# Expert rows added into the result by DMA, filler products in the first routing, later transposes, root degrees spread by a load: one graph transformer kernel on one core

## The chip, the cores and the metric

The kernel runs on one NeuronCore of one Trainium2 chip. The metric is the device time of one execution in microseconds (us). The kernel before was timed three times: 1880.01, 1882.05 and 1882.09 us, median 1882.05. One further execution was profiled.

## The reference, cut to what matters

There are N = 1250 nodes with C = 768 features and 20000 edges. Two layers are computed. Each adds to x a graph part and an attention part, both from the normalised x, and then a mixture of experts on the normalised result:

```
xn = layernorm(x)
x = x + gat(xn, edges) + linear_attention(xn)            # layer 0
x = x + experts0(layernorm(x))     # 8 experts, 2 per row, out = sum of gate * (row @ W_e + b_e)
xn = layernorm(x)
x = x + gcn(xn, edges) + l2_attention(xn)                # layer 1
x = x + experts1(layernorm(x))     # 8 experts, 2 per row, with a hidden layer and gelu
```

In `gcn` the row of every node is scaled by 1/sqrt(degree), on the source side and on the destination side. In `l2_attention` q and k are normalised over the nodes, so that their sums over all nodes are wanted beside them.

## The kernel before, in words

The 1250 rows are 10 tiles of 125 rows (`NT`, `T`). `X` holds x in SBUF, `XN` three normalised tiles, `XT` the transposed normalised rows. Work is written out by hand for each engine; semaphores tie them. `plan_jobs` numbers the jobs that go through PSUM and gives each a bank in turn and the engine that empties it; TensorE's `begin(m)` waits until the job that last had the bank was emptied. SP issues nearly all loads, in order; `load(u)` fills one of two weight slots of 2304 KB.

**Order in time.** Layer 0's k, v, q and projection run to 430 us, the graph part of layer 0 (units of two heads and some tiles, VectorE lines 1867 and following) to 728 us. During that part the tiles 0 to 7 are normalised for the experts (`normal(1, t)`), tiles 8 and 9 right after it (`LATE`).

**First routing** (`route`, TensorE L1020, VectorE L1901). VectorE picks two experts of each row; TensorE counts ranks (L1026 to L1028), VectorE makes from them the place of each row among tiles of 128 rows that belong to one expert, TensorE gathers the row numbers of each place into `TOK` (L1034, 20 products behind VectorE's L1956). `TAB` holds the expert of each tile and the numbers of turns. Between its products TensorE has nothing to do. With these inputs there are 25 tiles: 12 turns of two and one over.

**First experts** (TensorE L1042 `turn`, L1066 `expert0`). For tile n POOL gathers 128 normalised rows from DRAM (`gather`, L611, L622) into one of two buffers `XG`. TensorE transposes them (L1054), ScalarE copies them to `XGT` (L1404), TensorE multiplies by the expert's weights (L1076, 12 matmuls, which the profile shows as 24 passes). VectorE adds the bias to `YS` (L2011), ScalarE stores the 128 rows to DRAM in `expert_rows` (`store`, L1411). POOL forms the index of the gather itself: a multiplication (L614), a drain, a cast (L616), a drain, the indirect DMA (L622). After the last tile POOL gathers for every node tile the two rows of `expert_rows` that belong to its nodes (L657, 20 gathers, four buffers `YG`), and VectorE adds them to `X` with their gates `GW` (`weighted`, L2017), takes the statistics (L1578 to L1586) and normalises the tile (L1590, L1600) once ScalarE has the root (L1246).

**Next stage.** TensorE sums the degrees (L1099, L1104), transposes tiles 0 and 1 (L721) and computes q in five chunks of 250 nodes, six groups of 128 columns each (L1117, 12 passes a group); in each chunk, after three groups, it transposes the two tiles of the next chunk. A chunk waits until ScalarE has copied its two tiles. Then k and v follow (L744). VectorE has made for each tile a diagonal matrix `DG` of 1/sqrt(degree), and TensorE multiplies ones by it (L1126), which spreads the values over all partitions; VectorE copies them to `DB` (L2080). Then comes the projection (L734 with `QK`), whose start waits until VectorE has emptied v's last job.

**Second experts** (L1186, L1208). Here the gates are applied in place: twenty products (L1221) bring the three bf16 parts of the gates and the row numbers to each place, VectorE sums them (`GTE`, `SIDX`, L2165 to L2172), forms `YS` = gate * bias (L2000) and `YS` += gate * product (L2005), and POOL adds the rows of `YS` into the result in DRAM by an indirect DMA with addition (`add_rows`, L668). The indices of the gathers are made by VectorE (L2158). Two adds never run together: each waits for the one before it to land.

Of the kernel before, what the change touches and what calls it, by code (L numbers as in the profile page):

```python
# [13 lines left out]
P = 128  # L14
N = 1250
# [62 lines left out]
YB = {1: 4}  # L78
# [25 lines left out]
def plan_jobs():  # L104
# [27 lines left out]
    for L in (1, 2, 3):  # L132
# [34 lines left out]
def graph_transformer(nc, xn_d, y_d, x, src, dst, gW, gWT, gWresT, attnT, w0, wp0, bp0, rwT, rb, ewT, eb,  # L167
# [6 lines left out]
    def sb(name, shape, dt=F32):  # L174
# [35 lines left out]
    IDXA = sb("IDXA", [T, KT], U32)  # L210
# [135 lines left out]
    TVG = sb("TVG", [T, KT, 4, ETC], BF16)  # L346
    GTE = sb("GTE", [P, ETC])
    SIDX = sb("SIDX", [P, ETC])
    cursor[0] = eb_base
# [5 lines left out]
    YS = sb("YS", [P, 2, C])  # L355
    assert cursor[0] <= at_base
# [12 lines left out]
    YG1 = sb("YG1", [T, YB[1], C])  # L369
    assert cursor[0] <= top - XNB * C * 4  # L370
    cursor[0] = yg_base
# [22 lines left out]
    DG = sb("DG", [T, NT, T])  # L394
    assert cursor[0] <= top - XNB * C * 4
# [8 lines left out]
    consts = sem("consts")  # L404
# [17 lines left out]
    tn_filled, tn_emptied, lr_filled, lr_emptied, lg_filled, lg_emptied, dg_ready = (sem(s) for s in (  # L422
        "tn_filled", "tn_emptied", "lr_filled", "lr_emptied", "lg_filled", "lg_emptied", "dg_ready"))
# [4 lines left out]
    y_cleared = sem("y_cleared")  # L428
# [5 lines left out]
    yg_in, yg_used = [sem(f"yg_in{b}") for b in range(YB[1])], sem("yg_used")  # L434
    gate_parts, gates_full, gates_in, ys_ready, acc_in, idx_ready = (sem(s) for s in (
        "gate_parts", "gates_full", "gates_in", "ys_ready", "acc_in", "idx_ready"))
# [37 lines left out]
    def _(sp):  # L474
# [64 lines left out]
        spare = 2 * N // P * P  # L539
        sp.dma_start(y_d[spare:, :], x[0:ET_MAX * P - spare, :]).then_inc(y_cleared, 16)  # L540
# [6 lines left out]
        for u, (c, p) in enumerate(UNITS):  # L547
# [3 lines left out]
            if u >= RSLOTS:  # L551
                sp.wait_ge(w_ready, 20 * (u - RSLOTS + 1))
            sp.dma_start(RBS[u % RSLOTS][:, :, 0:nt * T],
                         rows_d[2 * p:2 * p + 2, t0 * T:(t0 + nt) * T].partition_broadcast(T)).then_inc(rb_in[u % RSLOTS], 16)
        sp.wait_ge(fin_dve, len(UNITS))
# [21 lines left out]
        for t in range(NT):  # L577
            sp.wait_ge(dve_emptied, J.emptied("dve", J.at[f"agg2_{t}"] + 1))
            sp.dma_start(out[t * T:t * T + PA, :], X[0:PA, t, :]).then_inc(acc_in, 16)
            sp.dma_start(out[t * T + PA:(t + 1) * T, :], X[PA:T, t, :]).then_inc(acc_in, 16)  # L580
# [7 lines left out]
        sp.wait_ge(acc_in, 32 * NT)  # L588
# [3 lines left out]
    def _(pool):  # L592
# [48 lines left out]
        with nc.gpsimd.Fori(0, n) as i:  # L641
            for a in range(2):
                pool.wait_ge(turned_n[1], i * 2 + a + 2)
                gather(1, i * 2 + a + 2, a)
        with nc.gpsimd.Fori(0, over) as j:
            pool.wait_ge(turned_n[1], n * 2 + j + 2)
            gather(1, n * 2 + j + 1, 0)

        pool.wait_ge(xg_in[1][0], (n + over) * 16 + 16)
        pool.wait_ge(xg_in[1][1], n * 16 + 16)  # L650
        pool.wait_ge(ys_out[1][0], (n + over) * 16 + 16)
        pool.wait_ge(ys_out[1][1], n * 16 + 16)
        nc.gpsimd.sem_inc(y_all, 1)
        for q in range(KT):
            if q >= YB[1]:
                pool.wait_ge(yg_used, q - YB[1] + 1)
            nc.gpsimd.indirect_dma_start(out=YG1[:, q % YB[1], :], out_offset=None, in_=y_d,  # L657
# [1569 lines left out]
```

## Time and profile before

| what | value |
| --- | --- |
| median of three runs | 1882.05 us |
| the profiled execution's own time | 1882.65 us |
| its span (first to last instruction) | 1880.7 us |
| mean granted clock of TensorE | 0.972 |
| TensorE busy | 1769.1 us (94%) |
| VectorE, ScalarE, POOL busy | 725.2, 392.5, 134.1 us |
| TensorE, share of the chain that ended last | 84% |
| bytes moved by DMA | 142.22 MB |

A page or an answer of the trace gives times in us from the first instruction, and durations of single instructions in us or ns. PE is TensorE, PEld its weight loads, DVE VectorE, ACT ScalarE, POOL GpSimd, SP the engine that issues loads; L with a number is a line of the kernel. The granted clock is a share of 2.4 GHz: 1.00 or 0.50, between them for a stretch with both. In the chain that ended last, each piece is what released the piece after it.

### The profile page before, as it was taken

How to read it: one execution, taken by the hardware profiler on the slowest of the kernel's cores; microseconds unless marked ns; L12 is line 12 of the kernel's file. 1: busy time of each engine (PE TensorE's matmuls, PEld its weight loads, DVE VectorE, ACT ScalarE, POOL GpSimd, SP SyncE). 2: the span in 40 equal slices, each digit the busy share in tenths (PEclk: the TensorE clock that was granted, in tenths of full speed). 3: DMA queues.
4: the chain of work that ended last, by engine and by line, in shares of the span. 5: the costliest groups of instructions: out<-in, count | busy, mean ns of one | idle time of the engine just before them, and what ended most of it. 6: DMA issues, size and time to landing. Idle time of an engine off the chain costs nothing.

```text
span 1880.7 us, 24731 instructions
## 1 busy us (share of the span) xinstructions
PE 1769.1 (94%) x7994; PEld 1090.2 (58%) x7995; DVE 725.2 (39%) x1826; ACT 392.5 (21%) x1034; POOL 134.1 (7%) x169
## 2 busy tenths in 40 slices
PE   7999999999999986899997999999999999779997
PEld 4555555554333343566666855555569669756664
DVE  4321545756789887211116211151111114432222
ACT  2441221113322222011013321000221221122221
POOL 0000000000000000111114000000000000013322
PEclk9999999999999998899998999999999999879999
DMA  6001101001001114355536011010010012535772
GB/s 196 1 0 62 68 24 39 1 1 36 30 23 49 34 42 182 95 200 190 195 130 190 30 51 51 0 51 0 0 51 1 0 50 84 193 105 139 198 196 40
DMA packets 53582, 142.22 MB, mean 76 GB/s; under 512 B 10079, under 2 KB 20723, under 8 KB 53045
## 3 DMA queue, kind: packets, MB, share of 16 engines
q1 hardware_dynamic: 34053, 87.05, 13.4%
q0 software_dynamic: 11952, 34.05, 7.5%
q10 hardware_dynamic: 7488, 19.93, 3.0%
q8 instruction: 56, 0.92, 0.2%
q14 instruction: 33, 0.27, 0.0%
HBM read 113.69 MB, written 33.99 MB: 79 GB/s over the span
## 4 chain that ended last, share of the span: by engine, by line
PE 84%; DVE 8%; issue 2%; DMA 2%; DVEq 2%; ACT 1%; ACTq 0%; POOL 0%; SPq 0%; POOLq 0%
PE PS L734 21%; PE PS L1076 10%; PE PS L744 8%; PE PS L1186 5%; PE PS L1208 5%; PE PS L842 4%; PE PS L876 4%; PE PS L1158 4%; PE PS L1144 4%; PE PS L1117 4%; PE PS L982 3%; DVE WRA L1867 3%; PE PS L823 2%; PE PS L1054 2%; PE PS L991 2%
## 5 line engine op out<-in xcount | busy, mean ns | idle before, releaser
L734 PE MATMUL PS<-WS,XT 128*125 128x384 f32 x960 | 313.6, 488 | 1.4 <-issue 1.4
L734 PEld LDWEIGHTS PS<-WS,XT 128*125 128x125 f32 x960 | 180.5, 189 | 129.5 <-issue 3.6
L1076 PE MATMUL PS<-WS,XGT 128*128 x600 | 199.4, 490 | 0.0
L1076 PEld LDWEIGHTS PS<-WS,XGT 128*128 128x128 f32 x600 | 113.1, 192 | 74.4 <-issue 2.0
L744 PE MATMUL PS<-XT,WS 128*128 128x416 f32 (+1 forms) x432 | 151.2, 512 | 0.0
L1867 DVE SCALAR_TENSOR_TENSOR WRA<-RB,U,AT 125x500 f32<-125x500 f32 (+1 forms) x240 | 140.0, 645 | 2.2 <-PE PS L991 0.6
L744 PEld LDWEIGHTS PS<-XT,WS 128*128 128x128 f32 x432 | 81.6, 189 | 69.2 <-issue 69.2
L982 PE MATMUL PS<-WRA,F 125*64 125x500 f32 (+1 forms) x480 | 100.7, 531 | 9.7 <-DVE WRA L1867 8.6
L1186 PE MATMUL PS<-WS,XGT 128*128 x288 | 99.4, 496 | 1.5 <-ACTq L1406 1.1
L2011 DVE TENSOR_TENSOR YS<-PS,EBB 128x768 f32<-128x768 f32 x25 | 23.9, 957 | 191.2 <-PE PS L1076 191.2
L1208 PE MATMUL PS<-WS,HT 128*128 x276 | 92.9, 486 | 1.0 <-DVE YS L2005 1.0
L1404 ACT ACTIVATE XGT<-PS 128x384 f32<-128x384 f32 x102 | 44.5, 488 | 222.8 <-DVE YS L2011 176.2
L876 PE MATMUL PS<-WS,QT 128*125 128x384 f32 x240 | 82.8, 499 | 0.0
L842 PE MATMUL PS<-XT,WS 128*128 128x416 f32 (+1 forms) x216 | 80.4, 525 | 0.5 <-DVEq L1730 0.5
L1117 PE MATMUL PS<-XT,WS 128*128 128x250 f32 x360 | 79.4, 382 | 0.6 <-issue 0.6
L626 POOL DMA_INDIRECT XG<-xn_rows,IDX x25 | 27.6, 1104 | 724.9 <-DVEq L1962 619.1
L1481 ACT ACTIVATE HF<-PS,DT 125x384 f32<-125x384 f32 x40 | 23.2, 581 | 263.0 <-PE PS L734 263.0
L734 PE MATMUL PS<-WS,QK 128*125 128x384 f32 x240 | 77.6, 486 | 0.0
L2094 DVE TENSOR_TENSOR HH<-HF,HH 125x384 fp32r<-125x384 f32 x40 | 22.3, 558 | 136.5 <-ACT HH L1483 136.5
L1117 PEld LDWEIGHTS PS<-XT,WS 128*128 128x128 f32 x360 | 69.5, 194 | 9.4 <-issue 1.0
L1186 PEld LDWEIGHTS PS<-WS,XGT 128*128 128x128 f32 x288 | 53.9, 194 | 35.0 <-issue 4.0
L1208 PEld LDWEIGHTS PS<-WS,HT 128*128 128x128 f32 x276 | 52.4, 190 | 37.6 <-issue 1.3
(319 smaller groups left out, 2149.6 us busy)
## 6 DMA issues: line engine op xcount, KB each, us to landing
WS<-in_ewT SPq DMA_DIRECT2D x8, 2304.0 KB, 10.6
WS<-in_fW SPq DMA_DIRECT2D x16, 1152.0 KB, 6.8
WS<-in_w SPq DMA_DIRECT2D x5, 2304.0 KB, 10.5
expert_rows<-YS ACTq DMA_DIRECT2D x25, 384.0 KB, 2.3
xn_rows<-XN ACTq DMA_DIRECT2D x20, 336.0 KB
RB<-expert_rows SPq DMA_DIRECT2D x12, 488.3 KB
WS<-in_wp SPq DMA_DIRECT2D x2, 2304.0 KB, 8.3
WS<-in_W SPq DMA_DIRECT2D x2, 2304.0 KB, 8.7
```

The lines of the kernel that those rows point to most:

```text
L734: last = nc.tensor.matmul(ps[0:T, 0:HC], lhsT[:, k, t * T:(t + 1) * T], w[:, k, b * HC:(b + 1) * HC], start=(k == 0), stop=(k == KC - 1))
L744: last = nc.tensor.matmul(ps[:, 0:n], w[:, k, q * P:(q + 1) * P], rhs[:, k, o:o + n], start=(k == 0), stop=(k == KC - 1))
L842: last = nc.tensor.matmul(ps[:, 0:n], w[:, k, q * P:(q + 1) * P], XT[:, k, o:o + n], start=(k == 0), stop=(k == KC - 1))
L876: last = nc.tensor.matmul(ps[0:T, 0:HC], QT[:, k, t * T:(t + 1) * T], w[:, k, b * HC:(b + 1) * HC], start=(k == 0), stop=(k == KC - 1))
L982: last = nc.tensor.matmul(num[j * D:(j + 1) * D], F[:, s, 2 * p + j, 0:D], WR[k % WSLOTS][:, j, 0:n], start=(s == 0), stop=(s == NT - 1), ...
L1076: last = nc.tensor.matmul(PS[:, 4 + 2 * a + b, 0:HC], XGT[:, a, k, :], WS[:, bass.ds(slot, 1), k * C + b * HC:k * C + (b + 1) * HC].rearra ...
L1117: last = nc.tensor.matmul(ps[:, 0:n], w[:, k, q * P:(q + 1) * P], XT[:, k, o:o + n], start=(k == 0), stop=(k == KC - 1))
L1144: last = nc.tensor.matmul(ps[:, 0:n], HH[:, v, s, q * P:(q + 1) * P], AT[:, s, o:o + n], start=(s + v == 0), stop=(s == NT - 1 and v == 1))
L1158: last = nc.tensor.matmul(ps[0:T, 0:HC], AT[:, s, t * T:(t + 1) * T], HH[:, v, s, b * HC:(b + 1) * HC], start=(s + v == 0), stop=(s == NT ...
L1186: last = nc.tensor.matmul(PS[:, 2 + a, 0:FH], XGT[:, a, k, :], WS[:, bass.ds(slot, 1), k * FH:(k + 1) * FH].rearrange("p a b -> p (a b)"), ...
L1208: last = nc.tensor.matmul(PS[:, 5 + b, 0:HC], HT[:, k, :], WS[:, bass.ds(slot, 1), o:o + HC].rearrange("p a b -> p (a b)"), start=(k == 0) ...
L1867: V.scalar_tensor_tensor(out=WR[k % WSLOTS][:, j, 0:nt * T], in0=RBS[u % RSLOTS][:, j, 0:nt * T], scalar=U[:, s, h:h + 1], in1=AT[:, s, t0 ...
```

## The change

1. **The first experts' rows are added into the result tensor.** `X` is stored to the result while the graph part runs (tiles 0 to 7) and before the expert loads (8 and 9). The gates are applied in the first experts as in the second: `gate_terms` and `gate_rows` on VectorE, `gate_products` on TensorE after the first tile, and `add_rows` on POOL for each tile, between the gathers. The store on ScalarE, the clearing load of `expert_rows`, the 20 gathers on POOL and `weighted` on VectorE are gone; after the last add SP loads the ten tiles of `X` back.
2. **Products of constants** (`kept_busy`): 18 matmuls of ones before the ranks, 19 after them, 19 after the tokens, in a spare bank.
3. **Transposes behind five groups** instead of three, in each chunk of q.
4. **Root degrees by a load.** VectorE's reciprocal is stored to DRAM (1250 single values) and loaded back with every partition reading the same row.

```diff
@@ plan_jobs
-                j.add(f"q1a_{c}", [a] * 3)
+                j.add(f"q1a_{c}", [a] * 5)
...
-                j.add(f"q1b_{c}", [a] * 3)
+                j.add(f"q1b_{c}", [a])
             j.add("v1", [v] * 18)
-            j.add("dinv", [v] * 3)
@@ SP
-        spare = 2 * N // P * P
-        sp.dma_start(y_d[spare:, :], x[0:ET_MAX * P - spare, :]).then_inc(y_cleared, 16)
+        def rows_out(t):
+            sp.dma_start(out[t * T:t * T + PA, :], X[0:PA, t, :]).then_inc(acc_in, 16)
+            sp.dma_start(out[t * T + PA:(t + 1) * T, :], X[PA:T, t, :]).then_inc(acc_in, 16)
...
+            if u - 4 in LN1_IN:
+                sp.wait_ge(xn_ready, NT + LN1_IN[u - 4] + 1)
+                rows_out(LN1_IN[u - 4])
...
         sp.dma_start(EBB1, eb.partition_broadcast(P)).then_inc(eb_in, 16)
+        for t in range(LATE, NT):
+            sp.wait_ge(xn_ready, NT + t + 1)
+            rows_out(t)
         expert_loads(1, U_EW, U_MIX1)
+        sp.wait_ge(acc_in, 32 * NT)
+        sp.wait_ge(y_all, 1)
+        for t in range(NT):
+            sp.dma_start(X[0:PA, t, :], out[t * T:t * T + PA, :]).then_inc(x2_in[t], 16)
+            sp.dma_start(X[PA:T, t, :], out[t * T + PA:(t + 1) * T, :]).then_inc(x2_in[t], 16)
...
         sp.wait_ge(stage_done, 2)
+        sp.wait_ge(dt_ready, 1)
+        sp.dma_start(inv_rows[0].rearrange("(t p) -> p t", p=T), DT, allow_slow_non_contiguous=True).then_inc(drow_out, 16)
+        sp.wait_ge(drow_out, 16)
+        sp.wait_ge(pe_filled, J.filled(J.at[f"lnt2_{NT - 1}"] + 1))
+        sp.dma_start(DB, inv_rows[0].partition_broadcast(P)).then_inc(db_in, 16)
@@ POOL
+        def add_rows(L, n, a, landed):
+            pool.wait_ge(ys_ready[L], n + 1)
+            for b, count in landed:
+                pool.wait_ge(ys_out[L][b], count * 16)
+            nc.gpsimd.sem_inc(pool_step, 1)
+            nc.gpsimd.indirect_dma_start(out=out, out_offset=bass.IndirectOffsetOnAxis(ap=SX[:, a:a + 1], axis=0),
...
+                                         compute_op=ALU.add).then_inc(ys_out[L][a], 16)
...
+        with nc.gpsimd.Fori(1, n) as i:
+            pool.wait_ge(turned_n[1], i * 2 + 3)
+            gather(1, i * 2 + 3, 1)
+            add_rows(1, i * 2, 0, [(1, i)])
+            pool.wait_ge(turned_n[1], i * 2 + 4)
+            gather(1, i * 2 + 4, 0)
+            add_rows(1, i * 2 + 1, 1, [(0, i + 1)])
+        with nc.gpsimd.Fori(0, over) as j:
+            pool.wait_ge(turned_n[1], n * 2 + j + 2)
+            pool.wait_ge(xg_in[1][0], (n + j) * 16 + 32)
+            gather(1, n * 2 + j + 1, 0)
+            add_rows(1, n * 2 + j, 0, [(1, n), (0, n + j)])
...
-        for q in range(KT):
...
-            nc.gpsimd.indirect_dma_start(out=YG1[:, q % YB[1], :], out_offset=None, in_=y_d,
@@ TensorE
+        def kept_busy(n, b):
+            for i in range(n):
+                nc.tensor.matmul(PS[:, b, 0:P], ones, ones, start=True, stop=True)
...
+            if L == 1:
+                kept_busy(18, spare)
             pe.wait_ge(sel_ready, k)
...
+            if L == 1:
+                kept_busy(19, spare)
             ps = begin(J.at[f"tokens{L}"])
...
             last.then_inc(pe_filled, 1)
+            if L == 1:
+                kept_busy(19, spare)
...
         turn(1, 0, 0, 16)
-        with nc.tensor.Fori(0, turns1) as i:
+        turn(1, 1, 1, 16)
+        expert0(0, 0)
+        gate_products(1)
+        turn(1, 2, 0, 32)
+        pe.wait_ge(gates_in, 1)
+        expert0(1, 1)
+        with nc.tensor.Fori(1, turns1) as i:
...
-                if q == 3 and c + 1 < len(QC):
+                if q == 5 and c + 1 < len(QC):
...
-        pe.wait_ge(dg_ready, 1)
-        for q in range(3):
-            ps = begin(J.at["dinv"] + q)
...
@@ ScalarE
-        def store(n, a):
-            act.wait_ge(y_free[1], n + 3)
-            act.dma_start(y_d[bass.ds(n * P, P), :], YS[:, a, :]).then_inc(ys_out[1][a], 16)
...
-                if q == 3:
+                if q == 5:
@@ VectorE
+            gate = GTE[:, bass.ds(n, 1)] if not isinstance(n, int) else GTE[:, n:n + 1]
+            if not isinstance(i, int):
+                dve.wait_ge(ys_out[L][a], i * 16)
+            V.tensor_scalar(YS[:, a, :], EBB[L][:, bass.ds(e, 1), :].rearrange("p a c -> p (a c)"), gate, None, ALU.mult)
+            V.tensor_copy(SX[:, a:a + 1], SIDX[:, bass.ds(n, 1)])
+            V.drain()
             dve.wait_ge(y_filled[L], n + 2)
...
+            V.drain().then_inc(ys_ready[L], 1)
...
+        gate_terms(TVG[1])
         dve.wait_ge(eb_in, 16)
...
+        gate_rows(1)
+        for a in range(2):
+            expert_rows(1, a, a, 0)
+        with nc.vector.Fori(1, turns1) as i:
...
         for t in range(NT):
-            weighted(t, 0)
-            V.drain()
-            weighted(t, 1)
-            if t >= 3:
+            if t:
                 normal(2, t - 1)
-            V.drain()
+            dve.wait_ge(x2_in[t], 32)
             spread_of(2, t)
...
-        for t in range(NT):
-            V.tensor_scalar(DG[:, t, :], ident[0:T, 0:T], DT[:, t:t + 1], None, ALU.mult)
...
-            V.tensor_copy(DB[:, 4 * q * T:(4 * q + w) * T], ps[:, 0:w * T]).then_inc(dve_emptied, 1)
```

`gate_terms` splits the gates into three bf16 parts and multiplies each by the one-hot places; `gate_rows` sums the three products and forms the row numbers. Both are the second experts' lines, now called twice.

## Rows read from the trace of the kernel before

**Rows 1.** the page, part 4: the chain that ended last, by engine
```profile
PE 84%; DVE 8%; issue 2%; DMA 2%; DVEq 2%; ACT 1%; ACTq 0%; POOL 0%; SPq 0%; POOLq 0%
```

**Rows 2.** chain that ended last, 940 to 1100: start us, us, what
```profile
958.29 15.48 PE PS L1076 x48
...
975.65 4.46 DMA expert_rows<-YS
...
982.61 7.26 DMA YG<-expert_rows,IDXA
...
1012.51 15.19 PE PS L1117 x72
```

**Rows 3.** timeline 958 to 1075: start, us, engine, line, tiles, [idle before]
```profile
997.18 0.68 DVE L1600 TENSOR_SCALAR XN<-X,mv,rstd 125x768 f32<-125x768 f32 x1
...
1000.47 10.41 PE L1117 MATMUL PS<-XT,WS 128*128 128x250 f32 x36 [0.62 <-issue]
```

**Rows 4.** windows: length, busy PE, PEld, DVE, ACT, POOL, granted clock, DMA share, GB/s
```profile
742.00:743.00 1.00, 0.00 (x0) 0.00 (x0) 0.75 (x4) 0.00 (x0) 0.00 (x0) 0.94 1.02 409
...
1005.00:1006.00 1.00, 1.00 (x4) 0.81 (x4) 0.91 (x3) 0.00 (x0) 0.67 (x1) 0.65 0.85 207
```

**Rows 5.** timeline 710 to 765, TensorE in the first routing
```profile
744.71 0.30 PE L1026 MATMUL PS<-SEL,before 125*125 125x80 bf16 x1 [4.99 <-issue]
...
750.83 3.23 PE L1034 MATMUL PS<-TV,OHR 125*128 125x60 bf16 x20 [5.66 <-DVE OHR L1956]
...
759.55 1.54 PE L1054 MATMUL PS<-ident,XG 128*128 128x128 f32 x6 [5.50 <-DMA XG<-xn_rows,IDX]
...
761.57 1.54 PE L1054 MATMUL PS<-ident,XG 128*128 128x128 f32 x6 [0.47 <-DMA XG<-xn_rows,IDX]
...
763.07 9.82 PE L1076 MATMUL PS<-WS,XGT 128*128 x24
```

**Rows 6.** chain, then timeline, around 1236: end of the v stage
```profile
1235.77 2.23 PE PS L1126 x20
...
1235.81 0.65 DVE L2074 SCALAR_TENSOR_TENSOR QK<-PS,SC,QK 128x416 f32<-128x416 f32 x1 [3.54 <-PE PS L744]
```

**Rows 7.** timeline 1630 to 1690, last experts: products and last sum
```profile
1666.12 1.22 PE L1221 MATMUL PS<-TVG,OHR 125*128 125x120 bf16 x20
...
1668.37 0.18 DVE L2172 TENSOR_TENSOR GTE<-GTE,PS 128x30 f32<-128x30 f32 x1
```

**Rows 8.** timeline 1860 to 1881, then all 23 adds of L668: landing
```profile
1861.02 1.02 DVE L2005 SCALAR_TENSOR_TENSOR YS<-PS,GTE,YS 128x768 f32<-128x768 f32 x1 [0.94 <-PE PS L1208]
...
1863.07 1.57 POOL L668 DMA_INDIRECT out_x<-YS,SX  x1 [7.18 <-DVEq L2007]
...
DMA to landing us min/median/max: 4.9/5.6/6.4
```

**Rows 9.** timeline of POOL, of SP; landing of the gathers of 762.79 and 833.87
```profile
767.13 0.18 POOL L616 CAST IDX<-IDXF 128x1 uint32<-128x1 f32 x1 [3.14 <-issue]
768.08 0.98 POOL L622 DMA_INDIRECT XG<-xn_rows,IDX  x1 [0.76 <-issue]
...
841.84 0.18 POOL L616 CAST IDX<-IDXF 128x1 uint32<-128x1 f32 x1 [0.74 <-issue]
...
831.71 0.37 SPq L491 DMA_DIRECT2D WS<-in_ewT  x1
...
DMA to landing us min/median/max: 4.2/4.2/4.2
...
DMA to landing us min/median/max: 7.8/7.8/7.8
```

**Rows 10.** timeline 0 to 20: VectorE, first statistics and second normalised tile
```profile
8.39 1.02 DVE L1578 BATCH_NORM_STATS2 stats<-X 125x6 f32<-125x384 f32 x2 [1.50 <-DMA X<-in_x]
...
13.07 0.68 DVE L1600 TENSOR_SCALAR XN<-X,mv,rstd 125x768 f32<-125x768 f32 x1
```

**Rows 11.** tile YG: the issues of its 20 gathers on POOL, ns min/median/max
```profile
L657 POOL DMA_INDIRECT YG<-expert_rows,IDXA x20: 1180/1202/1990, 981.1 to 1031.7; - x20
```

More of the change, by code:

```diff
@@ L640, in _ @@
         over = nc.gpsimd.value_load(TAB[0:1, 2, 1:2], min_val=1, max_val=2)
[L641 to L653, printed above, removed]
-        for q in range(KT):
-            if q >= YB[1]:
-                pool.wait_ge(yg_used, q - YB[1] + 1)
-            nc.gpsimd.indirect_dma_start(out=YG1[:, q % YB[1], :], out_offset=None, in_=y_d,
-                                         in_offset=bass.IndirectOffsetOnAxis(ap=IDXA[:, q:q + 1], axis=0)
-                                         ).then_inc(yg_in[q % YB[1]], 16)
-        def add_rows(n, a, landed):
-            pool.wait_ge(ys_ready, n + 1)
+        def add_rows(L, n, a, landed):
+            pool.wait_ge(ys_ready[L], n + 1)
             for b, count in landed:
-                pool.wait_ge(ys_out[3][b], count * 16)
+                pool.wait_ge(ys_out[L][b], count * 16)
             nc.gpsimd.sem_inc(pool_step, 1)
@@ L1055, in turn, with gate_products @@
             last.then_inc(turned_n[L], 1)
+        def gate_products(k):
+            pe.wait_ge(gate_parts, k)
+            tvg = TVG[1 if k == 1 else 3]
+            for q in range(KT):
+                last = nc.tensor.matmul(PS[:, 7, 0:4 * ETC], OHR[:, q, :], tvg[:, q, :, :].rearrange("p a b -> p (a b)"),
+                                        start=(q == 0), stop=(q == KT - 1))
+            last.then_inc(gates_full, 1)
         def weights_of(L, n, u0):
@@ L1121, in _ @@
             columns(J.at[name], weights(U_MIX1 + n), XT)
-        pe.wait_ge(dg_ready, 1)
-        for q in range(3):
-            ps = begin(J.at["dinv"] + q)
-            for t in range(4 * q, min(4 * q + 4, NT)):
-                last = nc.tensor.matmul(ps[:, (t % 4) * T:(t % 4 + 1) * T], ones[0:T, :], DG[:, t, :], start=True, stop=True)
-            last.then_inc(pe_filled, 1)
         w = weights(U_MIX1 + 3)
@@ L1218, in _ @@
         hidden(0, 0)
-        pe.wait_ge(gate_parts, 1)
-        for q in range(KT):
-            last = nc.tensor.matmul(PS[:, 7, 0:4 * ETC], OHR[:, q, :], TVG[:, q, :, :].rearrange("p a b -> p (a b)"),
-                                    start=(q == 0), stop=(q == KT - 1))
-        last.then_inc(gates_full, 1)
+        gate_products(2)
         with nc.tensor.Fori(0, turns3) as i:
@@ new lines, in expert_rows, with gate_terms @@
+            V.drain().then_inc(ys_ready[L], 1)
+        def gate_terms(tvg):
+            V.drain()
+            V.tensor_copy(GPB[:, 0], GW)
+            V.drain()
+            V.tensor_tensor(GR, GW, GPB[:, 0], ALU.subtract)
+            V.drain()
+            V.tensor_copy(GPB[:, 1], GR)
+            V.drain()
+            V.tensor_tensor(GR, GR, GPB[:, 1], ALU.subtract)
+            V.drain()
+            V.tensor_copy(GPB[:, 2], GR)
+            V.drain()
+            terms = tvg.rearrange("p (t k) v e -> p t k v e", k=2)
+            for n in range(2):
+                ot = OT.rearrange("p (t k) e -> p t k e", k=2)[:, :, n, :]
+                for m in range(3):
+                    V.tensor_tensor(terms[:, :, n, m, :], ot, GPB[:, m, n, :].unsqueeze(2).to_broadcast([T, NT, ETC]), ALU.mult)
+            V.tensor_copy(tvg[:, :, 3, :], OT)
+            V.drain().then_inc(gate_parts, 1)
@@ L2075, in _ @@
                                    op0=ALU.mult, op1=ALU.mult).then_inc(dve_emptied, 1)
-        for q in range(3):
-            ps = full(J.at["dinv"] + q)
-            w = min(4 * q + 4, NT) - 4 * q
-            V.tensor_copy(DB[:, 4 * q * T:(4 * q + w) * T], ps[:, 0:w * T]).then_inc(dve_emptied, 1)
-        V.drain()
         dve.wait_ge(mix_bias, 48)
```

165 lines of the change are left out of this document (69 added, 96 removed).

## The prediction

> **What bounds the kernel now.** The page first: TensorE holds 84% of the chain that ended last [rows 1], so a saving counts only where TensorE waits or runs at its lower clock. The edits touch three places of that chain. *Between the first experts and the next stage*: the last expert's matmuls end at 973.8; then follow the store of its rows (4.46 us), the gather of the first rows back (7.26) [rows 2], and the second normalised tile, ready at 997.86; the q matmuls begin at 1000.47 [rows 3]. That is 26.7 us in which TensorE has only the degree sums and four half transposes. *The routing before the experts*: the granted clock is still up in most of the microsecond from 742, then at half (1.2 GHz) into the first tile; after the experts it is at half again until it returns within the microsecond from 1005 [rows 4]. So the first expert tile takes 9.8 us [rows 5] where two later ones take 15.48, 7.74 each [rows 2]. *The root degrees*: twenty matmuls, 2.23 us, on the chain [rows 6].
>
> The sum is made against the profiled execution, 1882.65 us (its span 1880.70 and 1.95 around it). It lies 0.60 above the median of 1882.05, and the last line is on the median. I count within 0.2% (1878.3 to 1885.8) as no change.
>
> **Products of constants in the routing.** 18, 19 and 19 f32 matmuls, each two passes of 128 columns. A pass with the same weights and 125 columns takes 2.23/20 = 0.11 us [rows 6], so a batch costs 4.1 to 4.3 us at full clock. TensorE idles 4.99, 5.66 and 5.50 us before the ranks, the tokens and the first rows' transposes [rows 5]; the batches fit there, at nothing on the chain. What they buy: if the clock stays up, the six transposes at 761.57, which wait for their gather and not for the clock, take about 0.65 instead of 1.54 (the half clock doubles them), so the experts start at 762.2 instead of 763.1, and the first tile takes 7.74 instead of 9.8: −2.9. Without the cover (half clock) a batch takes 8.5 us: the third would then delay the experts by some 3 us. Between these I take the gain, since the first batch starts at full clock.
>
> **Gates in the first experts.** After the first tile come twenty bf16 matmuls (1.22 us), and before the second tile the wait for VectorE's five small operations, in the last experts from their end at 1667.34 to the sum of the gates at 1668.55, 1.2 us [rows 7], 0.65 of it under the third transposes: +1.8. The gates' splitting on VectorE before them has the whole first tile to hide under, 7.7 us; even twice the last experts' work from routing to products would fit, so nothing. So the second tile starts at 772.4 instead of 773.5: −1.1 for this and the part above. It reaches the end through the first add, below, and is not counted twice. A tile then costs VectorE two passes over its rows (one of 1.02 us [rows 8], one shorter) under 8.4 us of TensorE: nothing. ScalarE loses its store: nothing.
>
> **The adds on POOL.** This decides the case. Before, POOL only gathers: its index is formed in two small operations with a drain between, and it has 8.4 us for it. Now every tile also has an add, issued from the same queue, one at a time. In the last experts such an add is issued 1.03 us after VectorE's end (1862.04 to 1863.07) and lands a median of 5.6 us after issue (4.9 to 6.4) [rows 8]. What is queued behind it is the next gather, with its drain. One place shows what a drain does there: a gather issued at 762.79 lands 4.2 us later, at 766.99, and the index copy behind the drain starts only at 767.13; again, one issued at 833.87 takes 7.8, to 841.67, and the copy starts at 841.84 [rows 9]. So the drain waits for the queue's transfer to land. That it also waits for one that adds into DRAM no row shows; I take it as likely. Then one round of POOL is landing 5.6 + 0.14 + copy 0.18 + gap 0.77 + gather's issue 0.98 + 0.3 to the next add = 8.0 us, say 8.1 with the loop's registers: just under TensorE's 8.39 (7.74 + 0.65). But seven times in this stage 2.3 MB of weights are loaded, issued as a tile ends (831.71), and the gather behind that one is the one of 7.8 us instead of about 4 [rows 9]. An add is issued 2.4 us after the tile's end, inside that load. Bounds of its stretch: nothing (in the last experts, beside loads of half the size, 4.9 to 6.4 was all) and 3.9 us (the gather's, less its quiet time); I take 1.7, since such an add is long by latency and its range there is narrow. A round beside a load is then 9.8.
> First add: the first tile ends at 769.9, products 1.2, gates 1.2, both passes 2.0, then 1.1: issued at 775.5. The last is 24 rounds later: 775.5 + 24 × 8.1 + 7 × 1.7 = 981.8. Were POOL no limit, it would be issued at 972.6 + 2.4 = 975.0. So the stage slips by 6.8 us, partly as waits of TensorE for gathered rows, partly as adds that trail.
>
> **The reload.** Last add lands 981.8 + 5.6 = 987.4. POOL's and SP's signals 0.7 (two semaphore steps of 0.3). The first tile of X (375 KB): no such load stands alone in the trace. Bounds: its bytes alone (0.9 at the 409 GB/s of [rows 4]), and the last store of that size, 4.46 [rows 2]. The nearest row is the gather of the same bytes, 4.2, of which 0.98 is POOL's issue [rows 9]: 3.2. I take 3.0. Then two tiles through VectorE and ScalarE as at the kernel's start, 8.39 to 13.75 = 5.4 us [rows 10], and transposes and copies 2.2 to 2.6 as before (997.86 to 1000.47): q starts at 998.7 instead of 1000.5, −1.8. TensorE's own line (rows of the last gather, degree sums 6 to 8 us, columns 3) ends near 997: under this. Beside it go the 20 gathers and 20 weighted sums; nobody waits for them any more. The later tiles load at under 1 us each and are used at 2.8 us each: hidden.
>
> **Transposes after five groups.** The first chunk's 36 passes end at 1000.47 + 10.41 = 1010.88 [rows 3]; 72 passes take 15.19 from 1012.51 [rows 2], so with 1.28 us of transposes TensorE waited 0.35 for the fourth normalised tile. Five groups give that 12.7 us: −0.4. ScalarE's copies (1.6 us) now hide under one group (2.5) instead of three: nothing, 0.9 to spare. The 2.6 us that the lower clock costs here (half of 1000.5 to 1005.7) I leave as it is; if the degree sums come right before, it is gained as well.
>
> **Root degrees by a load.** −2.23, but TensorE now meets VectorE's last product (1235.81 + 0.65, after matmuls that end at 1235.77) [rows 6]: −1.4. The scattered store, the broadcast load and two waits on SP stand near 1040 to 1062, ahead of the biases and of a weight load not issued before TensorE's q stage ends near 1083: nothing; uncovered, they would cost some microseconds on SP alone.
> **Stores of X** (20 on SP): issue 0.3 to 0.4 us each, between loads that have two units of slack; the last two tiles add 0.75 MB behind the biases, 1.8 us of bytes, done near 756, before the first gather's bytes: nothing. POOL waits for them and for the gates before its first add; queued behind is the gather of the fifth tile, issued near 782 and landed by 787, which TensorE wants at 788.6: nothing, with 2 us to spare.
>
> Sum: −1.8 − 0.4 − 1.4 = −3.6: 1879.05 against the profiled run, **1878.4** on the median.
>
> A rule that speaks against the change: in the last gathers of this stage the issue takes 1.18 to 1.99 us [rows 11], long where a VectorE operation on two SBUF operands had begun before it. The Trainium skill, page "SBUF — State Buffer", section "SBUF: two separate sides", says that VectorE and GpSimd share a port pair, held for a whole instruction, so that descriptors can't be written under some VectorE operations; the trace agrees with its 1.99 us.
>
> **The rivals.**
> 1. *The drain doesn't wait for an add.* Then adds run beside gathers, POOL never binds, no slip, and the last add at 975.0 starts q at 992.0: −8.5 − 0.4 − 1.4 = −10.3, 1871.7. For it: the drains seen stood behind gathers only. 0.25.
> 2. *Slower: POOL's round above TensorE's.* With the gather's stretch of 3.9 at seven adds and rounds of 8.25, the last add is issued at 775.5 + 198 + 27.3 = 1000.8, a slip of 25.8 against 6.8: 19.0 more, +15.4, 1897; at 2.9 and 8.2 the slip is 17.6, +7.2, 1889. It decides once the slip passes 6.8 + 3.6 = 10.4 us. 0.17.
> 3. *VectorE holds POOL's port.* The scaled biases (0.62 us) start as an add lands, just as POOL forms its index. At most 0.6 in each of 24 rounds: 14 more, 1892; the copy and the issue mostly straddle it. 0.04. By the skill's rule this is a full block whenever they meet.
> 4. *The clock isn't held* in the routing: the batches don't do what they are for, and the first tile starts up to 3 us late at half clock. POOL's chain starts 4 us later: 1882. 0.06.
>
> My forecast has 0.48: 1874 to 1884.
> Range: 1870 to 1890, from just under rival 1 to the middle of rival 2. Faster: all of rival 1, 0.29 of my own case (1878.3 cuts it just below its middle, and its errors lean down: a shorter landing acts 24 times), 0.01 of the rest: 0.55. Same: 0.19 of my own, 0.04 each of rivals 4 and 2, 0.01 of rival 3: 0.28. Slower: 0.17.
>
> **What the profile after would show.** Right: L614 to L616 on POOL idle 4 to 5 us in every tile, TensorE's transposes waiting for gathers by 5 us in all, the last add near 982, L1117 starting near 999, no L1126. The clock at 1.0 from 740 to 985. Wrong: index copies that start before the add has landed and a last add at 975 (rival 1); waits of TensorE for XG above 12 us (rival 2); a first tile above 9 us (rival 4). The forecast falls with the landing time of an add: 0.1 us more is 2.4 us at the end.

## The result, and the profile after

| | before | after |
|---|---|---|
| median of the runs, us | 1882.09 | 1890.0 (7 runs, 1884.98 to 1893.53) |
| ratio to before | | 1.0037, 95% interval 1.0022 to 1.0053 |
| both again, in a later set of runs (E9) | 1881.6 | 1890.91, ratio 1.0056 (1.0041 to 1.0072) |
| profiled execution, span | 1882.65, 1880.7 | 1885.56, 1883.5 |

The changed kernel is slower, by 7 to 10 us, where 3.6 us less were forecast. Its profiled execution, 1885.56 us, is the second fastest of its seven, so the profile falls short of the medians; the table further down shows where.

The chain that ended last of the changed kernel, by engine (it answers [rows 1]: "issue" was 2%, and POOL's sequencer, POOLq, was not in it):

```profile
PE 75%; issue 9%; DVE 8%; POOLq 3%; DVEq 2%; DMA 2%; ACT 1%; ACTq 0%; POOL 0%; SPq 0%
```

The routing and the first tile, in the timeline (start, us, engine, line, tiles, idle before), which answer [rows 5]. L748 is the products, L1095 the first transposes, L1125 the first tile:

```profile
745.86 3.23 PE L1073 MATMUL PS<-TV,OHR 125*128 125x60 bf16 x20 [1.32 <-DVE OHR L1989]
748.91 5.81 PE L748 MATMUL PS<-ones 128*128 128x128 f32 x38
...
754.91 0.87 PE L1095 MATMUL PS<-ident,XG 128*128 128x128 f32 x6 [0.19 <-issue]
756.48 0.87 PE L1095 MATMUL PS<-ident,XG 128*128 128x128 f32 x6 [0.70 <-DMA XG<-xn_rows,IDX]
...
757.74 8.00 PE L1125 MATMUL PS<-WS,XGT 128*128 x24 [0.38 <-issue]
```

The batches of products fit, the transposes take 0.87 us instead of 1.54, the tile 8.00 instead of 9.82. But everything is also 5 us earlier than in the kernel before, and that began long ahead of any part that was costed.

Two rounds of POOL, from the same timeline (L668 the add, L636 the index copy behind the drain, L642 the gather; they answer [rows 8, 9]), and the scaled bias of VectorE (L2030) beside one of them:

```profile
940.63 0.62 DVE L2030 TENSOR_SCALAR YS<-EBB,GTE 128x768 f32 x1 [2.67 <-DMA out_x<-YS,SX]
940.68 0.60 POOL L636 CAST IDX<-IDXF 128x1 uint32<-128x1 f32 x1 [6.52 <-issue]
...
943.40 1.60 POOL L668 DMA_INDIRECT out_x<-YS,SX  x1 [0.30 <-issue]
...
949.53 0.18 POOL L636 CAST IDX<-IDXF 128x1 uint32<-128x1 f32 x1 [4.31 <-issue]
...
950.51 1.04 POOL L642 DMA_INDIRECT XG<-xn_rows,IDX  x1 [0.81 <-issue]
...
951.86 1.60 POOL L668 DMA_INDIRECT out_x<-YS,SX  x1 [0.30 <-issue]
```

The copy starts 6.13 us after the add's issue, when the add has landed; that is also the median over the 24 rounds. From the copy to the next add it is 2.3 to 2.7 us. The view of those two lines, for the 26 copies and for the 25 adds of this stage:

```profile
L636 POOL CAST IDX<-IDXF x26: 178/185/605, 756.7 to 983.7; 128x1 uint32<-128x1 f32 x26
...
  issue: 113.8, 26
```
```profile
DMA to landing us min/median/max: 5.3/5.8/9.3
```

The 113.8 us of "issue" ahead of the copies stand where the drain is: POOL waits for nothing that the profile can name. That it is the drain, E5 shows. The adds run from 771.61 to 986.01, 24 rounds of 8.93 us; in the second profile of this kernel from 769.35 to 983.59, again 8.93. Eighteen of the rounds lie between 8.02 and 8.68 us, the six others between 9.10 and 12.20. Five of these lie beside a weight load; two of the seven loads stretched no round.

Behind the last add, the chain that ended last (start, us, what):

```profile
981.06 2.66 issue
...
984.70 4.15 DMA XG<-xn_rows,IDX
...
988.90 1.55 PE PS L1095 x6
...
991.50 8.65 PE PS L1154 x30
1000.15 0.02 issue
1000.18 0.52 ACT DROW L1477
...
1000.83 2.32 PE PS L1159 x20
...
1003.47 0.21 ACT std L1291
...
1003.94 0.68 DVE XN L1633
...
1009.44 2.84 PE PS L1172 x6
```

It does not pass the last add or the reload of X at all. It passes the last gather (whose rows no tile uses; no run leaves it out), which POOL issues at 984.70 because its drain waits for an add. TensorE stands behind it 5.64 us, then makes the degree sums at a lower clock (8.65 us, 5.97 in the kernel before). ScalarE takes the root of the first tile's variance (L1291) only behind the degrees' own root. That tile's variance had been ready since 996.45:

```profile
996.30 0.15 DVE L1619 TENSOR_SCALAR std<-mv 125x1 f32<-125x1 f32 x1
...
1003.70 0.16 DVE L1623 RECIPROCAL rstd<-std 125x1 f32<-125x1 f32 x1 [7.25 <-ACT std L1291]
```

The granted clock in this stretch (windows, columns as [rows 4]) is 0.64 during the degree sums and 0.50 when q starts:

```profile
991.00:1000.00 9.00, 8.50 (x30) 8.03 (x30) 1.38 (x4) 1.45 (x4) 0.00 (x0) 0.64 0.84 233
...
1005.00:1010.00 5.00, 3.26 (x14) 2.43 (x13) 3.50 (x12) 2.01 (x6) 0.00 (x0) 0.50 0.26 79
```

### The profile page after: what moved, and what is told of

Its sections match the earlier page's. It is cut to its first block, busy times and chain, and to the rows that moved or that the text cites. A ratio compares the mean times of both kernels' runs of the same rounds, so it can differ in the third digit from the quotient of the medians.

```text
span 1883.5 us, 25088 instructions
## 1 busy us (share of the span) xinstructions
PE 1780.5 (95%) x8106; PEld 1099.3 (58%) x8107; DVE 724.6 (38%) x1860; ACT 392.3 (21%) x1034; POOL 153.5 (8%) x177
## 4 chain that ended last, share of the span: by engine, by line
PE 75%; issue 9%; DVE 8%; POOLq 3%; DVEq 2%; DMA 2%; ACT 1%; ACTq 0%; POOL 0%; SPq 0%
PE PS L768 21%; PE PS L778 8%; PE PS L1235 5%; PE PS L1257 5%; PE PS L1172 4%; PE PS L911 4%; PE PS L877 4%; PE PS L1207 4%; PE PS L1193 4%; PE PS L1017 3%; DVE WRA L1900 3%; POOLq L635 2%; PE PS L858 2%; PE PS L1026 2%; DVE WRB L1900 1%
## 5 line engine op out<-in xcount | busy, mean ns | idle before, releaser
L1125 PE MATMUL PS<-WS,XGT 128*128 x600 | 198.8, 488 | 6.9 <-issue 2.6
L1125 PEld LDWEIGHTS PS<-WS,XGT 128*128 128x128 f32 x600 | 112.1, 190 | 82.8 <-issue 9.4
L2035 DVE SCALAR_TENSOR_TENSOR YS<-PS,GTE,YS 128x768 f32<-128x768 f32 x48 | 48.8, 1017 | 159.4 <-PE PS L1125 142.0
L668 POOL DMA_INDIRECT out_x<-YS,SX x48 | 76.9, 1602 | 65.8 <-DVEq L2037 45.2
```

What stands on the lines that cost most here:

```text
L668: nc.gpsimd.indirect_dma_start(out=out, out_offset=bass.IndirectOffsetOnAxis(ap=SX[:, a:a + 1], axis=0), in_=YS[:, a, :], in_offset=None, ...
L1125: last = nc.tensor.matmul(PS[:, 4 + 2 * a + b, 0:HC], XGT[:, a, k, :], WS[:, bass.ds(slot, 1), k * C + b * HC:k * C + (b + 1) * HC].rearra ...
```

## Twelve experiments

Each time stands with its ratio to the kernel before, run on the same chip; 0.001 is 1.9 us. The changed kernel is taken at 1.0046, the middle of its two ratios, some 8.7 us above before.

**Where do the 5 us before the experts come from?** In the kernel before the chain shows a stall of TensorE at 192.85, then four products of the next stage at half clock:

```profile
186.63 6.22 PE PS L799 x205
192.85 2.44 issue
195.29 1.28 PE PS L799 x35
...
197.32 3.05 PE PS L842 x4
```

In the changed kernel the same 240 products run through:

```profile
185.88 7.24 PE PS L834 x240
...
193.88 6.19 PE PS L877 x17
```

The DMA queues of the kernel before from 186 to 197 us:

```profile
q1 hardware_dynamic: 1753, 3.59, 98.9%
q8 instruction: 1, 0.02, 0.5%
```

The clearing load fills them, and one instruction block (16 KB, its own queue) comes; in the changed kernel, in the same window, two come:

```profile
q1 hardware_dynamic: 285, 0.01, 1.3%
q8 instruction: 2, 0.03, 1.3%
```

E1 moved that load in the kernel before; it was then issued at 272.9 us instead of 186.2.

```diff
-        sp.dma_start(y_d[spare:, :], x[0:ET_MAX * P - spare, :]).then_inc(y_cleared, 16)
         unit_left(1)
         sp.wait_ge(at_ready, WQ)
         load(3)
+        sp.dma_start(y_d[spare:, :], x[0:ET_MAX * P - spare, :]).then_inc(y_cleared, 16)
```

> The kernel before, with the 3.4 MB load that clears rows of the scratch tensor issued after the fourth weight load (near 300 us) instead of at 180 us; nothing else differs. Theory: in the kernel before, this load fills the DMA queues from 186 to 197 us, an instruction block (16 KB, the instruction queue) comes late behind it, TensorE waits 2.44 us for nothing that the profile shows, and its clock then falls to half; so its removal, and not the parts I costed, made the changed kernel 3.4 us earlier by 194 us. Expected: 3 to 4 us faster than before (near 1878.5), first L842 product near 194 instead of 197.3. Rival: the 2.44 us are chance of that one profiled run; then no difference over 0.5 us in the median. If the load does the same harm at its new place, the gain is given back there, near 300 us.

Measured: 1876.2 us, ratio 0.9969 (0.9958 to 0.998). TensorE runs without the stall, the next stage starts at 193.6, the graph part at 431.5 (before 436.5, changed kernel 431.6). Shown: the load's place costs 5 to 6 us in the medians (3.8 to 7.9 by the interval). In the profile it is 4.1 of the 5.0 us, since 1.0 lay ahead of the load already (the 240 products start at 185.6 instead of 186.6). That is more than the stall alone, because the clock falls behind it: four products of 0.76 us there against 17 of 0.36. This is the changed kernel's gain too, so its other parts lose some 14 us and not 9.

Two more profiles bear out that the stall is no chance of one execution. The kernels of E10 and E12, below, keep the load in its place, and both stall behind the same 205 passes:

```profile
195.57 1.27 PE L805 MATMUL PS<-VR,KR 125*64 125x65 f32 x35 [2.40 <-issue]
...
195.60 2.22 PE L805 MATMUL PS<-VR,KR 125*64 125x65 f32 x35 [3.55 <-issue]
```

In these three profiles the instruction block comes at 192.95 to 193.22 us, and TensorE goes on 1.4 us after it is in, however long it has stood. In the eleven profiles without the load there, the block comes at 188.1 to 189.7 and nothing stalls. So I take it that TensorE waited for that block; that it comes late because the queues are full is inferred.

**Is it POOL's drain?** E2 gives the row numbers to VectorE, as the last experts have it. `gather`, which multiplies, drains, casts and drains on POOL, is called no more; `gather1` only waits and issues. VectorE makes each index ahead of a tile's scaled bias. One of the calls stands here for all:

```diff
+        def gather1(k, b):
+            pool.wait_ge(idx1_ready, k)
+            nc.gpsimd.sem_inc(pool_step, 1)
+            fetch(1, b)
...
-            pool.wait_ge(turned_n[1], i * 2 + 3)
-            gather(1, i * 2 + 3, 1)
+            gather1(i * 2 + 2, 1)
...
+        def row_index1(m, b):
+            dve.wait_ge(turned_n[1], m)
+            V.tensor_copy(IDX[:, b:b + 1], TOK[:, bass.ds(m, 1)]).then_inc(idx1_ready, 1)
```

> The changed kernel, but the row numbers of the first experts' gathers are made by VectorE (one copy each, as the last experts have it), so that POOL has no drain between an add and the next gather. Theory (POOL binds by its drain behind the add): gathers now run beside adds, TensorE's round of 8.39 us sets the pace, the last add is issued near 972 instead of 986 us, lands near 977.5, the rows of X come back and the q products begin near 990 instead of 1009; time near 1867 to 1871, 18 us under the changed kernel and 11 to 15 under the one before, and a smaller spread from run to run. Rival A (adds and gathers together take the bandwidth or latency: landings grow to 8 us or more when they overlap): at most 3 us gained on the changed kernel, 1885 to 1890. Rival B (ScalarE's and TensorE's tail behind the last add holds the stage anyway): the last add is near 972 but q starts only near 1000, 1877 to 1881.

Measured: 1874.84 us (1869.95 to 1878.2), ratio 0.9961 (0.9946 to 0.9977): 16 us under the changed kernel. The timeline shows the gather 1.89 us behind the add's issue:

```profile
947.13 1.59 POOL L669 DMA_INDIRECT out_x<-YS,SX  x1 [5.61 <-issue]
...
949.02 0.99 POOL L643 DMA_INDIRECT XG<-xn_rows,IDX  x1 [0.30 <-issue]
```

24 rounds take 200.2 us, 8.34 each, the last add is issued at 971.66, q starts at 990.6. Adds landed in 5.6 us (median, longest 9.0) with gathers beside them, so rival A falls. The time in the middle is 4 us above what was expected and the spread is no smaller: three runs lie near 1870, four between 1874.8 and 1878.2, at a mean clock of 0.979 against 0.976 to 0.977. Where those four lose it no profile shows.

E5 is e2 with one drain put back in `gather1`, and none of the index work.

```diff
             pool.wait_ge(idx1_ready, k)
             nc.gpsimd.sem_inc(pool_step, 1)
+            pool.drain()
```

> The kernel of e2 (row numbers made by VectorE) with one drain put back on POOL ahead of each gather, and nothing else of the old index work. Theory (a drain on POOL waits until the add before it has landed): the gather's issue starts 5.5 to 6 us after the add's issue instead of 1.9 as in e2; but POOL's round is then only landing 5.6, gather 1.0, add's start 0.3 and small gaps, near 7.1 us, under TensorE's 8.39, so the last add stays within 4 us of e2's 971.7 and the time within 3 us of e2 (1872 to 1878 on a before of 1881.4). So the drain binds only together with the two index operations (copy, gap and second wait, 1.2 us) and loads beside it. Rival (the drain takes no notice of transfers in flight, and it is the index operations' own time or VectorE's port that held POOL): the gather's issue stays 1.9 to 2.1 us behind the add's.

Measured: 1883.39 us, ratio 1.0006 (0.9997 to 1.0015). The rival falls: the gather waits until the add has landed, 6.50 us behind its issue instead of 1.89:

```profile
774.66 1.61 POOL L669 DMA_INDIRECT out_x<-YS,SX  x1 [4.91 <-DVE IDX L2081]
781.16 0.99 POOL L643 DMA_INDIRECT XG<-xn_rows,IDX  x1 [4.89 <-issue]
782.46 1.59 POOL L669 DMA_INDIRECT out_x<-YS,SX  x1 [0.30 <-issue]
```

But the expected price was wrong: some 8.5 us over e2, not 3. A round is 7.8 us where it is quiet and not 7.1, and over the stage 8.66 (774.66 to 982.44), since rounds beside a load of weights take 9.6 to 11.8 and there is little room to catch up. Of the 16 us between e2 and the changed kernel the one drain is 8.5; what is left of the old index work (two operations and the second drain) is the rest, 7.5. The profiles put this in two places: the 24 rounds take 200.2, 207.8 and 214.4 us in e2, e5 and the changed kernel, and from the last add to the start of q it is 19.0, 22.8 and 23.4.

**What does the tail cost?** E3 moves ScalarE's first two roots forward.

```diff
             nc.scalar.activation(DROW[:, o:o + n], ps[0:1, 0:n], ACT.Copy).then_inc(deg_sum, 1)
             nc.scalar.drain().then_inc(act_emptied, 1)
+            if c:
+                root(2, c - 1)
...
         nc.scalar.drain().then_inc(act_emptied, 1)
-        root(2, 0)
-        root(2, 1)
         turned_tile(2, 0)
```

> The changed kernel, with ScalarE's roots of the first two normalised tiles issued behind the second and third copy of the degree sums instead of behind all three and the degrees' own root. Theory: in the changed kernel the first root waits 7 us in ScalarE's order behind the degree sums, which TensorE can begin only when the last gathered rows have come; with this order the first normalised tile is ready near 998 instead of 1004, q starts near 1004 to 1005 instead of 1009.4, 4 to 5 us faster than the changed kernel, about level with the one before (1880 to 1886 given the changed kernel's spread). Rival: TensorE is not free before 1003 anyway (degree sums, columns) and the degrees' root now comes later: 1 us gained or less, 1888 to 1890.

Measured: 1885.51 us, ratio 1.0023 (1.0012 to 1.0034), some 4 us under the changed kernel. In the trace the root comes 5.1 us earlier and q starts at 1005.1 instead of 1009.4; 1.3 us of that is the degree sums, which took 7.35 us here instead of 8.65:

```profile
998.33 0.20 ACT L1291 ACTIVATE std<-std 125x1 f32<-125x1 f32 x1
...
1005.08 7.21 PE L1172 MATMUL PS<-XT,WS 128*128 128x250 f32 x19 [0.62 <-issue]
```

**What are the products of constants worth?** E4 is the changed kernel without its 56 products, E8 is e2 without them (`kept_busy(...)` left out in the routing), E12 is the kernel before with them alone.

> The changed kernel without the 56 products of constants in the first routing (left out; they feed nothing). Theory: the clock falls to half at 742 us as in the kernel before, the first expert tile takes 9.8 us instead of 8.0 and its transposes 1.5 instead of 0.65, the first add is issued 2.9 us later, and since POOL's rounds follow one by one from the first add, the whole 2.9 us come through: 1892 to 1893 against the changed kernel's 1890. Rival: the chain does not start at the first tile (POOL catches up or the clock is not held for their sake): no difference, 1890.

Measured: 1888.2 us, ratio 1.0041 (1.0025 to 1.0056): no difference from the changed kernel. The first tile took 8.51 us, the first add came 2.0 us later (773.60), the last 1.2 (987.16). But 1.1 us of that lay ahead of the first batch: the transposes of tiles 8 and 9, the work before it, began at 730.52 instead of 729.39. Counted from them the first add is 0.9 us later and the last one not at all (256.6 us behind in both).

> The kernel of e2 without the 56 products of constants in the first routing (they feed nothing). e4 showed no cost of leaving them out while POOL set the pace. Theory: with POOL no longer binding, the 2 us by which the first add comes later reach the end: 2 to 3 us slower than e2 (near 1877). Rival: the products are worth nothing anywhere, no difference from e2 (1874.8).

Measured: 1871.14 us, ratio 0.9945 (0.9931 to 0.9958): not slower than e2. The clock is at half from 738 us, but comes back early in the first tile:

```profile
754.64 1.54 PE L1094 MATMUL PS<-ident,XG 128*128 128x128 f32 x6 [5.49 <-DMA XG<-xn_rows,IDX]
...
757.96 8.18 PE L1124 MATMUL PS<-WS,XGT 128*128 x24
...
769.56 5.75 PE L1124 MATMUL PS<-WS,XGT 128*128 x17 [1.70 <-ACTq L1450]
```

The second tile starts at 769.56, with the products at 768.99; counted from the transposes of tiles 8 and 9 it is 0.4 us later.

> The kernel before with the 56 products of constants in the first routing alone (they feed nothing). In the prediction they were worth 2.9 us there: first tile 7.8 instead of 9.8 us, transposes 0.65 instead of 1.5, and TensorE sets the pace of this stage in the kernel before, so the gain would reach the end: 1878.7 on a before of 1881.6. Rival (from e4 and e8, where the first tile took 8.5 and 8.2 us without any products): the clock comes back early in the first tile anyway and the products are worth 0.5 to 1.5 us, 1880 to 1881.

Measured: 1878.53 us, ratio 0.998 (0.9971 to 0.9989), 2.1 to 5.5 us faster. The median agrees with the term of 2.9 us; the profile shows only a third of it in its place. The tile took 8.00 us, but the first batch (5.67 us) and the third (7.10) ran in part at half clock. The first held the ranks back by 0.9 us, the third the transposes to 763.40. From the transposes of tiles 8 and 9 to the second tile it was 38.2 us, against 39.2 before: 1.0 us gained. A further 1.7 us lies between the last expert product and q, which this edit does not touch, and is not explained. In the changed kernel even less is there to gain: a tile without products took 8.2 to 8.5 us, not 9.8. Why the clock comes back sooner there is open. And a batch is not free: in three of the nine profiles with products (e5, e7, e12) the first one ran in 5.7 to 5.8 us instead of 4.3, and the ranks came 0.9 to 1.1 us later.

**The two small parts.** E10 is the kernel before with the transposes behind five groups and the root degrees by a load, both hunks of the diff as they are.

> The kernel before with the two small parts of the change alone: transposes of the next tiles behind five groups of q instead of three, and the root degrees spread by a store and a broadcast load instead of twenty matmuls. Prediction's terms: 0.4 and 1.4 us, 1.8 in all (from the start of q to the first aggregation product 392.4 instead of 394.2 us). Rival: the scattered store and the two waits on SP delay the weight loads behind them; then the distance is 394 or more.

Measured: 1879.87 us, ratio 0.9993 (0.9981 to 1.0004). From q to the first aggregation product 392.7 us (before 394.2, changed kernel 392.6): 1.5 us, as forecast but for 0.3. The median agrees (1.3 us), though its interval does not shut out zero.

**Is there a better kernel?** E6 is e2 with both roots ahead of the degrees' own root; E7 adds products in TensorE's gaps of the tail, E11 fewer of them: 8 for the 10 below, and 4 and 2 for the 20 and 8. The first two lines are E6's.

```diff
+        root(2, 0)
+        root(2, 1)
         ps = full(J.at["deg_cols"])
         nc.scalar.activation(DT, ps[0:T, 0:2 * NT:2], ACT.Sqrt).then_inc(deg_root, 1)
...
             expert0(n, 0, free=turns1 * 2 + j * 2 + 1)
+            pe.wait_ge(y_free[1], turns1 * 2 + 2)
+            kept_busy(10, 7)
...
+        kept_busy(5, 7)
         pe.wait_ge(xgt_ready[1], turns1 * 2 + over1 + 2)
...
         for t in (0, 1):
+            kept_busy((20, 8)[t], J.bank[J.at["lnt2_1"] + 1])
             transpose_tile(2, t, J.at[f"lnt2_{t}"])
```

> The kernel of e2 with ScalarE's two roots for the first normalised tiles ahead of the degrees' own root. Theory: in e2 VectorE still waited 2.67 us for its first root and the second tile came 2.6 us after it; q starts near 988 instead of 990.6, 1.5 to 2.5 us faster than e2 (1872 to 1873 on a before of 1881.4). Rival: TensorE's transposes wait for the columns of the degrees, half the gain or none.

Measured: 1872.44 us, ratio 0.9949 (0.9935 to 0.9963), q at 989.3: 1.7 us earlier than e2, counted from the first add; in the medians the difference is no more than the noise.

> The kernel of e6 with products of constants (10, 5, 20 and 8, they feed nothing) in TensorE's gaps behind the last expert tile: ahead of the last turn, of the degree sums, and of the first two tiles' transposes. Theory: in e2 the clock is at half from about 976 to 1005 us, so the degree sums took 7.38 us (5.97 at full clock in the kernel before), columns 2.65, two times six transposes 1.51 each, and the first 60 passes of q 14.42 instead of 12.7; with the clock held these give back 3 to 5 us: 1868 to 1870 on a before of 1881.4. Rival: the products delay real work by as much as the clock gives, no difference from e6.

Measured: 1870.51 us, ratio 0.9936 (0.9922 to 0.9949). In the profile no gain: the degree sums fell to 5.98 us and the first 60 passes of q to 12.89, but the batch of 20 stood in the way of the transposes.

```profile
975.35 5.98 PE L1156 MATMUL PS<-AT,onesr 125*128 125x418 f32 x30
...
984.34 6.24 PE L747 MATMUL PS<-ones 128*128 128x128 f32 x40
...
990.41 0.81 PE L754 MATMUL PS<-ident,XN 125*128 125x125 f32 x6
```

> The kernel of e7 with 8, 5, 4 and 2 products instead of 10, 5, 20 and 8. In e7 the batch of 20 began at half clock, took 6.24 us and held the first transposes back to 990.4, 5.8 us after their tile was near ready, while the degree sums fell from 7.38 to 5.98 us. Theory: keeping the products that cover idle time alone gives the degree sums' 1.4 us and costs the transposes 1 us at most: q starts near 990 to 991 counted against e7's 994.3, 1868 to 1870 on a before of 1882. Rival: with fewer products the clock falls before q starts and the first 60 passes take 15 us as in e6; level with e6 and e7, 1870 to 1873.

Measured: 1867.86 us (1865.65 to 1869.62), ratio 0.9935 (0.9919 to 0.9951), the fastest median of all, though by its ratio level with e7; about 12 us under the kernel before and 21 under the changed one. The transposes are free again, q starts at 987.9, and its first 60 passes take 12.89 us where e6 needed 15.32:

```profile
982.72 1.28 PE L747 MATMUL PS<-ones 128*128 128x128 f32 x8
983.79 1.46 PE L754 MATMUL PS<-ident,XN 125*128 125x125 f32 x6
...
987.88 12.89 PE L1175 MATMUL PS<-XT,WS 128*128 128x250 f32 x60 [0.62 <-issue]
```

In medians e11, e7 and e6 overlap; all three are faster than both kernels.

**The changed kernel again:**

> The changed kernel unaltered, on the same chip as the three that follow. From its first seven runs: 1.0037 of before (1884.98 to 1893.53). Theory (POOL's chain of drains, whose length varies with each landing, sets the stage): the last add is again near 985 to 990 us, 24 rounds of 8.8 to 9.0 us, q starts 18 to 20 us behind it through the tail. If instead the first profile was an unlucky one, its rounds would now be near 8.4 and the time under 1880.

Measured: 1890.91 us, ratio 1.0056 (1.0041 to 1.0072); last add at 983.59, q at 1007.1, 23.5 us behind it, rounds again of 8.93 us. The first profile was not an unlucky one.

## Why the prediction was wrong, step by step

Two terms of the sum failed, both in the stage of the first experts: the 24 rounds of POOL, whose size was wrong, and the way from the last add to q, where the forecast followed the wrong branch. Against the profiled execution, in the prediction's own terms:

| term | forecast | measured | difference |
|---|---|---|---|
| work ahead of the experts | 0 | 4.9 earlier | −4.9 |
| first add, by before's clock | 775.5 | 771.6 + 4.9 = 776.5 | +1.0 |
| 24 rounds of POOL | 206.3 | 214.4 | +8.1 |
| last add to start of q | 16.9 | 23.4 | +6.5 |
| q to first aggregation product | −1.8 | −1.6 | +0.2 |
| from there to the end | 0 | 481.5 against 486.0 | −4.5 |

Together +6.4, which is the step from −3.6 to the +2.8 of the two spans. The last row I take for chance and not for an effect of the change: in the fourteen profiles of this case that stretch took 481.5 to 486.6 us, the changed kernel at one end (484.6 in its second profile) and the kernel before near the other (482.1 in E10, which differs from it by two small parts). Without it the changed kernel is 7.3 us behind, near the 7.9 and 9.3 of its medians.

- **The adds on POOL: mechanism right, size wrong.** "That it also waits for one that adds into DRAM no row shows; I take it as likely" was right (e5). Mis-sized was "8.0 us, say 8.1": most rounds took 8.4 (18 of them 8.41 on average), because the wait behind an add is 6.13 us and not 5.74, and what follows it 2.3 to 2.7 and not 2.23. The six long rounds were 10.5 on average, for the "9.8" of seven beside a load. I had put 8.1 "just under" TensorE's 8.39 and given the slower rival 0.17 on "It decides once the slip passes 6.8 + 3.6 = 10.4 us"; the slip was 15.9 (990.9 by before's clock against 975.0). With 0.3 us between the two engines and 24 rounds, the two cases deserved about even chances: 0.1 us of a round was known to be 2.4 us at the end. The prediction's own sign of rival 2 came true: TensorE waited 24.4 us for gathered rows, for "above 12 us". That rival's 1889 lies so near the measured 1890 by luck in part: the 6.5 us of the tail and the 4.9 us of earlier work, which it had neither, nearly cancel.
- **"TensorE's own line ... ends near 997: under this": the step that failed in kind.** The line was worked out for TensorE alone. Its start hung on POOL's last gather, itself behind a drain, and its end (1003.15, 17.1 us behind the last add) did not hand over to the transposes but to ScalarE, in whose order the first tile's root stands behind the degree sums; q came another 6.3 us later. The reload that the forecast followed instead was right: the first tile's statistics began at 994.91, 8.9 us behind the last add, for a forecast of 9.3. Behind them VectorE waited 7.25 us for the root, and e3, which changes ScalarE's order alone, gave some 4 us back.
- **Products of constants: the median agrees where the term was worked out** (e12: 2.1 to 5.5 us for 2.9, of which its profile finds 1.0 in place), wrong in the changed kernel, where e4 and e8 show nothing lost without them. Rival 4 priced the clock's loss at a whole 4 us of POOL's chain; in e4 it was 0.9 at the first add and nothing at the last.
- **The clearing load, not costed at all.** The diff removes it, and I passed over it because nobody waited for it. The stall of 2.44 us in the chain that I read stood in the middle of its transfer. Its removal was the largest gain of the change (e1).
- **Transposes and root degrees: right,** 1.5 us by e10 for 1.8. **Gates: right within 2 us** (second tile by before's clock at 769.2 + 4.9 = 774.1, forecast 772.4).
- **Rival 3, VectorE on POOL's port,** exists in small: a copy of 0.60 us instead of 0.18 ends at 941.28, the scaled bias that began 0.05 us ahead of it at 941.25. The rule of the Trainium skill that the prediction cites (page "SBUF — State Buffer", section "SBUF: two separate sides") has the loser wait for the whole instruction, and this trace agrees. It is 0.3 to 0.4 us in six of the 24 rounds, 2.2 us in all, and so a part of the +8.1, not the 14 us of the rival.

The range, 1870 to 1890, ends where the result lies; the direction was the one given 0.17.

## What to carry to other kernels

Where an engine issues both adds and gathers, look at what stands between them: here a drain turned each landing into POOL's own time, and the index made on VectorE took that away. When a branch is set aside as "under" the critical one, follow it through every in-order queue it shares with it, ScalarE's too, before that is believed. And cost what a diff removes even if nobody waits for it: here a large transfer was paid for by an instruction block that came late.

## What was not expected of the hardware

- An instruction block of 16 KB came 3 to 5 us later beside a 3.4 MB transfer, and TensorE stood 2.40 to 3.55 us with nothing named (before, e10, e12); with the half clock behind it that was 5 to 6 us (e1).
- A drain on POOL waits for an indirect DMA that adds into DRAM: 6.50 us from the add's issue to the next gather's, 1.89 without it (e5, e2).
- Products of constants begun at half clock delayed the work they were to help: 40 passes took 6.24 us (38 take 4.49 at full clock), and q started 3.7 us later than in e6, counted from the first add. With 8 passes in the same gap it started 1.2 us earlier, and its first 60 passes took the same 12.89 us (e7, e11).
